# Nine weight conversions instead of twelve, the last six gate/up weight tiles cast by POOL during their load, and swapped keys made by the load instead of by the store

## The chip, the cores and the metric

The kernel runs on the 8 cores of one Trainium2 chip. Each core takes 2 of the 16 batches and runs the same program; there is no traffic between cores. The time of a run is that of its slowest core, in microseconds (us). A core has a matrix engine (TensorE, PE in the profile), a vector engine (DVE), a scalar engine (ACT), a general engine (POOL) and SyncE (SP); 16 DMA engines move data between HBM and the on-chip memory SBUF. SP and POOL each issue DMAs in the order of their own instruction streams: a DMA that waits for a semaphore holds up everything behind it on that engine.

## The reference, cut to what matters

```python
x   = x + layernorm(attention(layernorm(x), Mq, Mk, Mv))
# attention, 8 heads, keys of 64: scores = q @ k.T / 8, softmax over the QUERIES (axis=1),
#   out = att @ v, with v of 128 per head
wg, wu, wd = w_gate.astype(f32) / 127, w_up.astype(f32) / 127, w_down.astype(f32) / 127   # int32 inputs
x   = x + layernorm((silu(layernorm(x) @ wg.T) * (layernorm(x) @ wu.T)) @ wd.T)
# x: (16, 2048, 1024) float32; w_gate, w_up: (3072, 1024) int32; w_down: (1024, 3072) int32
```

The softmax runs over the queries of one position, so what this "attention" needs at a time is small: for each of the 16 groups G of 256 rows, tiles K of keys and values come by, 16 tiles per group, 256 in all.

## The kernel before, in words

The 4096 rows of a core are cut into 8 blocks of 512. The program has two parts.

**Projections, blocks 0 to 7.** Rows of x are loaded as tiles of 128 (T = 0 to 31), normalized (`ln1`, L264 on), transposed into `xnT` and multiplied with Wq, Wk, Wv. From T = 20 on the transpose is a DMA issued by SP (`P.flip`, L78); SP's order puts it among the loads and stores of the other work. A block has 16 units: 0 to 3 make queries, 4 to 7 keys, 8 to 15 values. Queries, keys and values are stored to HBM (`qk_d`, `v_d`), SP again. From block 4 on, score and value units of the attention (`s_unit`, `av_unit`) run between the halves of the projection units.

The keys are needed in two forms, since a score matmul uses 64 partitions at a time: as they are, and with the upper and lower 64 partitions swapped. `qk_unit` stores three pieces side by side in each 3072-wide row of `qk_d`: queries, keys, and, with two stores of 64 partitions, the swapped keys. `load_qk` (L384) loads the whole row with one DMA per group.

**FFN, blocks n = 0 to 7.** For each of 24 weight tiles ht, `gate_unit` and `up_unit` use the tile `wgu` (gate and up weights, 128 x 2048 bf16, four buffers), then 16 `down_unit` parts use all of `wd_sb`. Attention units run between the halves of these units as well. `load_wgu(i)` (L508) brings tile i, counted over all blocks; the first 24 are block 0's. It is called when up unit i - 4 is through. The first down unit waits for the last of the 12 loads of `wd_sb`.

**Weights.** The inputs are int32 and the matmuls want bf16. A DMA issued by POOL can change the type as it moves data. `convert(c)` (L647) turns two gate/up tiles, 2 MB of int32 in HBM, into 1 MB of bf16 in HBM (`gu_bf`), from where SP loads them in every block. There are 12 conversions: four in the first 64 units (after units 22, 30, 40, 50), six at (block, unit) = (4, 12), (5, 6), (6, 0), (6, 6), (6, 12), (7, 2), and the last two behind tiles 2 and 5 of the first FFN block. The down weights are converted on their way into SBUF by 12 DMAs behind tiles 7 to 21 of that block (`load_wd`), and stay there. Each of these is issued on POOL behind a wait for TensorE's count at that place.

The order on TensorE, DVE and ACT is written out by the program with a clock of its own, and no cost in it depends on DMAs.

Of the kernel before, what the change touches and what calls it, by code (L numbers as in the profile page):

```python
# [9 lines left out]
BF16 = mybir.dt.bfloat16  # L10
# [7 lines left out]
NHT = 24  # L18
# [9 lines left out]
QUIET = 5  # L28
MM = 0.216
SPACE = 1.6  # L30


class Program:
# [87 lines left out]
def build():  # L121
    nc = bass.Bass("TRN2", target_bir_lowering=False, dynamic_dma_scratch_size=16384)
# [4 lines left out]
    gu_hbm = nc.dram_tensor("gu", [NHT, 128, 2048], I32, kind="ExternalInput").ap()  # L127
    wd_hbm = nc.dram_tensor("wd", [NHT, 128, 1024], I32, kind="ExternalInput").ap()
    out_hbm = nc.dram_tensor("out", [NB, 2048, D], F32, kind="ExternalOutput").ap()
    gu_bf = nc.dram_tensor("gu_bf", [NHT, 128, 2048], BF16, kind="Internal").ap()  # L130
    qk_d = nc.dram_tensor("qk_d", [16, 128, 3072], BF16, kind="Internal").ap()
    v_d = nc.dram_tensor("v_d", [NB * 16, 128, 1024], BF16, kind="Internal").ap()

    es = ExitStack()
    P = Program(nc, es)
# [11 lines left out]
    q_qks = [P.sem(f"q_qks{i}") for i in range(NBLK)]  # L147
    q_vs = [P.sem(f"q_vs{i}") for i in range(4)]
    q_qk = [P.sem(f"q_qk{i}") for i in range(2)]
    q_v = [P.sem(f"q_v{i}") for i in range(6)]  # L150
    q_x1 = [P.sem(f"q_x1{i}") for i in range(8)]
    q_x2T = [P.sem(f"q_x2T{i}") for i in range(8)]
    q_conv = [P.sem(f"q_conv{i}") for i in range(12)]
    q_wgu = [P.sem(f"q_wgu{i}") for i in range(4)]
    q_wd = P.sem("q_wd")
    q_out = [P.sem(f"q_out{i}") for i in range(8)]

# [150 lines left out]
    qk_stored, v_stored = {}, {}  # L308

    def proj_units(blk, banks):  # L310

        par = blk % 2
        xT = xnT[par]
        qk_ev, v_ev = {}, {}
        turn = [0]

        def bank():
            turn[0] += 1
            return banks[turn[0] % len(banks)]

        def group(lhs, rhs, ready):
            name, ap = bank()
            done = None
            for dt in range(8):
                first = [bank_free.get(name), *ready] if dt == 0 else ()
                done = P.mm(ap, lhs(dt), rhs(dt), dt == 0, dt == 7, first, done=dt == 7)
                if dt == 3:
                    P.spent(4 * MM, 0.5)
            return name, ap, done

        def qk_unit(which, i):
            w, st = (wq, qst[par]) if which == 0 else (wk, kst[par])
            ready = [w_tok[which], *(xnT_tok[4 * blk + j] for j in range(4))]
            name, ap, done = group(lambda dt: w[:, 512 * dt + 128 * i:512 * dt + 128 * (i + 1)],
                                   lambda dt: xT[:, 512 * dt:512 * (dt + 1)], ready)
            dst = bass.AP(st, 256 * i, [[2048, 128], [1024, 2], [1, 256]])
            prev = [qk_stored[blk - 2]] if blk >= 2 else []
            qk_ev[i] = bank_free[name] = evac(dst, ap, done, *prev)
            if i == 3:
                ev = [qk_ev[n] for n in range(4)]  # L340
                row = 2 * blk * 128 * 3072
                if which == 0:
                    P.dma("sync", bass.AP(qk_d.tensor, row, [[3072, 128], [128 * 3072, 2], [1, 1024]]),
                          bass.AP(st, 0, [[2048, 128], [1024, 2], [1, 1024]]), q_qks[blk], *ev)
                    return
                P.dma("sync", bass.AP(qk_d.tensor, row + 1024,
                                      [[3072, 128], [128 * 3072, 2], [1, 1024]]),
                      bass.AP(st, 0, [[2048, 128], [1024, 2], [1, 1024]]), q_qks[blk], *ev)
                for half in range(2):
                    qk_stored[blk] = P.dma(  # L350
                        "sync", bass.AP(qk_d.tensor, row + 2048 + 64 * half * 3072,
                                        [[3072, 64], [128 * 3072, 2], [1, 1024]]),
                        bass.AP(st, 64 * (1 - half) * 2048, [[2048, 64], [1024, 2], [1, 1024]]),
                        q_qks[blk], *ev)

        def v_unit(j, c2):
            ready = [w_tok[2], xnT_tok[4 * blk + j]]
            name, ap, done = group(lambda dt: xT[:, 512 * dt + 128 * j:512 * dt + 128 * (j + 1)],
                                   lambda dt: wv[:, 1024 * dt + 512 * c2:1024 * dt + 512 * (c2 + 1)],
                                   ready)  # L360
            if j == 3 and c2 == 1:
                proj_done[blk] = done
            half, hh = j % 2, j // 2
            st = vst[2 * par + half]
            dst = bass.AP(st, 1024 * c2 + 128 * hh, [[2048, 128], [256, 4], [1, 128]])
            v_ev[j, c2] = bank_free[name] = evac(dst, ap, done, v_stored.get((blk - 2, half)))
            if hh == 1 and c2 == 1:
                b, k4 = blk // 4, blk % 4
                v_stored[blk, half] = P.dma(
                    "sync", bass.AP(v_d.tensor, (16 * b + half) * 131072 + 256 * k4,  # L370
                                    [[1024, 128], [2 * 131072, 8], [1, 256]]),
                    bass.AP(st, 0, [[2048, 128], [256, 8], [1, 256]]), q_vs[2 * par + half],
                    *(v_ev[half + 2 * a, c] for a in range(2) for c in range(2)))

        units = [lambda w=w, i=i: qk_unit(w, i) for w in range(2) for i in range(4)]
        units += [lambda j=j, c=c: v_unit(j, c) for j in range(4) for c in range(2)]
        return units
# [4 lines left out]
    x2T_tok, s_at = {}, [0.0]  # L382

    def load_qk(G):  # L384
        qk_tok[G] = P.dma("sync", qk[G % 2][:, :], qk_d[G, :, :], q_qk[G % 2],
                          qk_stored[G // 2], s_done.get(16 * (G - 2) + 15))

    def load_v(K):
        b, t = K // 128, K % 16
# [117 lines left out]

    def load_wgu(i):  # L508
        ht = i % NHT
        wgu_tok[i] = P.dma("sync", wgu[i % 4][:, :], gu_bf[ht, :, :], q_wgu[i % 4],  # L510
                           conv_tok[ht // 2], wgu_read.get(i - 4), *(xl_idle if i < 4 else ()))

    def gate_unit(n, ht):
        i = NHT * n + ht
        w, xT = wgu[i % 4], x2T[n % 2]
        for dt in range(8):
# [4 lines left out]
            if dt == 3:  # L521
                P.spent(4 * MM, 0.5)
        t_ = th[i % 2]
        tanh = P.act(lambda s: s.activation(t_[:, :], F[0][:, :], AF.Tanh, scale=1.0 / 254.0),  # L524
                     done, th_read.get(i - 2), *(th_idle if i < 2 else ()))

        def finish():
            bank_free["F0"] = gated[i] = P.dve(lambda v: v.scalar_tensor_tensor(  # L528
# [116 lines left out]
        turn(T)  # L645

    def convert(c, *waits):  # L647
        conv_tok[c] = P.dma("gpsimd", gu_bf[2 * c:2 * c + 2, :, :], gu_hbm[2 * c:2 * c + 2, :, :],
                            q_conv[c], *waits)

    wide = [(f"O{i}", Op[i // 2][:, 512 * (i % 2):512 * (i % 2 + 1)]) for i in range(4)]
    narrow = [(f"F{i}", F[i][:, :]) for i in range(2)]
# [6 lines left out]
    norm_at = {0: 4, 1: 5, 2: 6, 3: 7, 13: 8, 14: 9, 15: 10, 16: 11,  # L659
               25: 12, 26: 13, 27: 14, 28: 15, 34: 16, 36: 17, 38: 18, 40: 19}  # L660
    turn_at = {24: 8, 25: 9, 26: 10, 27: 11, 33: 12, 34: 13, 35: 14, 36: 15, 49: 16, 51: 17, 53: 18, 55: 19}
    early_conv = {22: 0, 30: 1, 40: 2, 50: 3}
    later_conv = {(4, 12): 4, (5, 6): 5, (6, 0): 6, (6, 6): 7, (6, 12): 8, (7, 2): 9}
    for u, unit in enumerate(first + rest):
        if u == 8:
            for T in range(4, 8):
# [44 lines left out]
        dst = bass.AP(wd, 2 * c * 1024, [[NHT * 1024, 128], [1024, 2], [1, 1024]])  # L711
        wd_tok[:] = [P.dma("gpsimd", dst, src, q_wd, *ramp_idle, *waits)]

    first_block = {2: lambda *w: convert(10, *w), 5: lambda *w: convert(11, *w)}
    for c in range(12):
        first_block[7 + 4 * c // 3] = lambda *w, c=c: load_wd(c, *w)

# [55 lines left out]
```

How the kernel before makes its waits and increments, by code:

```python
                def body(eng, ops=self.ops[name]):  # L105
                    seen = {}
                    for waits, fn, inc, amt in ops:
                        for s, v in waits:
                            if seen.get(s, 0) < v:
                                seen[s] = v
                                eng.wait_ge(self.h[s], v)
                        if fn is None:
                            continue
                        made = fn(eng)
                        if inc is not None:
                            made.then_inc(self.h[inc], amt)
```

## Time and profile before

| | us |
|---|---|
| median of 3 runs | 1765.6 |
| lowest, highest | 1762.24, 1766.82 |
| the profiled execution's own time | 1772.76 |
| its span, slowest core (4) | 1771.0 |
| fastest core of it (2) | 1747.3 |
| TensorE busy on core 4 | 1693.3 (96%) |

The span is the time from the first to the last instruction of a core; the run's time is a little longer. The profile page is that of core 4. The granted TensorE clock was 0.99 to 1.00 of full speed on every core. The DMA line of the page, which gives the mean busy share of the 16 DMA engines in 40 slices of 44 us, reads `9899999789934553465435543555255525441421`: the engines are near full in the first 11 slices, about 490 us, and half idle after that. DMA bytes are counted where they are written: a conversion or a load of down weights reads twice what the profile counts. Busy shares of different queues can overlap and add to more than one.

### The profile page before, as it was taken

The page shows a single profiled execution, that of the slowest core. Times are in us where ns is not written, and L with a number is a line of the kernel's source. Part 1 is how long each engine was busy: PE and PEld are TensorE (multiplying, and loading weights), DVE is VectorE, ACT ScalarE, POOL GpSimd, SP SyncE. Part 2 cuts the span into 40 slices and gives each one's busy share as a digit, 9 for nine tenths or more (in the row PEclk, how much of TensorE's full clock was granted, in tenths as well). Part 3 has the DMA queues.
Part 4 walks back from the last instruction along what each step waited for, and adds up shares of the span by engine and source line. Part 5 has one row for each costly group of instructions (what it writes and reads, how often), then busy time and mean ns, then how long its engine had stood idle before and what let it go on. Part 6 is the DMA issues. An engine that isn't in the chain of part 4 may idle for free.

```text
span 1771.0 us, 31869 instructions; the slowest of 8 cores (1747.3 to 1771.0 us)
## 1 busy us (share of the span) xinstructions
PE 1693.3 (96%) x10912; PEld 799.9 (45%) x10912; DVE 849.6 (48%) x1904; ACT 854.0 (48%) x1447; POOL 125.9 (7%) x245
## 2 busy tenths in 40 slices
PE   5999986998999999999999999999999999999997
PEld 2444442444444444444444444444444444444443
DVE  3434462535454545545454536463646354635433
ACT  3443553655545554555455545554555455552111
POOL 2110010001010001000010001000100010001000
PEclk9999998999999999999999999999999999999999
DMA  9899999789934553465435543555255525441421
GB/s 197 198 201 253 222 224 150 214 189 240 258 123 142 190 159 132 129 199 155 143 114 199 154 159 102 194 150 174 85 185 176 173 93 170 158 162 48 155 95 48
DMA packets 157518, 288.35 MB, mean 163 GB/s; under 512 B 56624, under 2 KB 75056, under 8 KB 156976
## 3 DMA queue, kind: packets, MB, share of 16 engines
q1 hardware_dynamic: 150400, 263.24, 48.5%
q0 software_dynamic: 6960, 23.07, 9.9%
q8 instruction: 91, 1.49, 0.3%
q14 instruction: 67, 0.55, 0.1%
HBM read 260.05 MB, written 50.33 MB: 175 GB/s over the span
## 4 chain that ended last, share of the span: by engine, by line
PE 83%; DVE 6%; DMA 5%; issue 2%; ACT 2%; SPq 1%; POOL 1%; DVEq 0%; POOLq 0%; ACTq 0%
PE F L71 58%; PE Op L71 17%; PE Sp L71 8%; DMA xnT<-xn 2%; DVE bnB L225 1%; DVE bnB L226 1%; DMA wgu<-gu_bf 1%; DMA wk<-mk 1%; ACT E L419 1%; ACT y L244 1%; SPq L78 1%; DMA wd_sb<-wd 1%; DVE th L528 1%; DMA xl<-x 0%; DVE mvB L227 0%
## 5 line engine op out<-in xcount | busy, mean ns | idle before, releaser
L419 ACT ACTIVATE E<-Sp 128x1024 bf16<-128x1024 f32 x512 | 523.8, 1023 | 625.9 <-PE Sp L71 625.7
L71 PE MATMUL F<-x2T,wgu 128*128 128x512 bf16 x3072 | 780.0, 380 | 20.3 <-DVE th L528 16.1
L71 PEld LDWEIGHTS F<-x2T,wgu 128*128 128x128 bf16 x3072 | 256.8, 98 | 307.6 <-issue 109.0
L71 PE MATMUL F<-wd_sb,hT 128*128 128x512 bf16 x1536 | 365.7, 380 | 0.7 <-DMA wd_sb<-wd 0.5
L71 PEld LDWEIGHTS Op<-vt,E 128*128 128x128 bf16 x4096 | 270.9, 98 | 122.5 <-issue 7.8
L71 PE MATMUL Op<-vt,E 128*128 128x128 bf16 x4096 | 313.7, 220 | 0.8 <-DVE vt L429 0.8
L528 DVE SCALAR_TENSOR_TENSOR th<-th,F 128x512 f32<-128x512 f32 x192 | 131.9, 687 | 259.8 <-ACT th L524 259.8
L551 DVE TENSOR_TENSOR hT<-th,F 128x512 bf16<-128x512 f32 x192 | 131.8, 686 | 180.1 <-PE F L71 176.2
L71 PEld LDWEIGHTS F<-wd_sb,hT 128*128 128x128 bf16 x1536 | 137.7, 98 | 157.3 <-issue 23.9
L71 PE MATMUL Sp<-qk 64*128 64x512 bf16 x1024 | 200.1, 387 | 2.4 <-ACT E L419 1.5
L429 DVE TENSOR_SCALAR vt<-vt,rsx 128x1024 bf16<-128x1024 bf16 x256 | 125.4, 490 | 53.9 <-DVE rsx L428 45.9
L524 ACT ACTIVATE th<-F 128x512 f32<-128x512 f32 x192 | 114.5, 596 | 73.3 <-PE F L71 73.0
L71 PEld LDWEIGHTS Sp<-qk 64*128 64x128 bf16 x1024 | 49.7, 92 | 216.0 <-issue 215.0
L419 ACT ACTIVATION_READ_ACCUMULATOR E<-Sp 128x1 f32 x512 | 99.6, 194 | 0.0
L248 DVE TENSOR_TENSOR x<-x,y 128x1024 f32<-128x1024 f32 x64 | 78.1, 1223 | 34.2 <-ACT y L244 33.7
L230 POOL TENSOR_TENSOR rsB<-vfB,mhalf 128x1 f32<-128x1 f32 x64 | 41.4, 647 | 572.4 <-DVE vfB L228 562.5
L584 DVE BATCH_NORM_STATS2 bnC<-y 128x6 f32<-128x512 f32 x64 | 44.3, 692 | 70.3 <-ACT y L577 67.7
L589 POOL TENSOR_TENSOR rsC<-vfC,mhalf 128x1 f32<-128x1 f32 x32 | 18.5, 578 | 702.4 <-DVE ssum L426 495.8
L244 ACT ACTIVATE y<-y,nbC,rsC 128x1024 f32<-128x1024 f32 x32 | 39.7, 1240 | 59.2 <-POOL nbC L240 57.6
L71 PE MATMUL F<-wv,xnT 128*128 128x512 bf16 x256 | 66.0, 380 | 0.4 <-DVE ssum L426 0.4
L579 DVE COPY y<-F 128x512 f32<-128x512 f32 x32 | 22.1, 690 | 81.0 <-PE F L71 80.9
L71 PE MATMUL Op<-wv,xnT 128*128 128x512 bf16 x256 | 56.7, 379 | 0.9 <-DVE kst L304 0.8
(65 smaller groups left out, 832.2 us busy)
## 6 DMA issues: line engine op xcount, KB each, us to landing
wgu<-gu_bf SPq DMA_DIRECT2D x192, 512.0 KB, 4.2
vt<-v_d SPq DMA_DIRECT2D x256, 256.0 KB, 4.6
xl<-x SPq DMA_DIRECT2D x32, 512.0 KB, 9.0
x<-x SPq DMA_DIRECT2D x32, 512.0 KB, 5.9
out<-x SPq DMA_DIRECT2D x32, 512.0 KB, 2.7
gu_bf<-gu POOLq DMA_DIRECT2D x12, 1024.0 KB, 14.4
qk<-qk_d SPq DMA_DIRECT2D x16, 768.0 KB, 6.1
v_d<-vst SPq DMA_DIRECT2D x16, 512.0 KB, 12.0
```

The lines of the kernel that those rows point to most:

```text
L71: "tensor", lambda t: t.matmul(out, lhsT, rhs, start=start, stop=stop),
L230: return P.pool(lambda g: g.tensor_tensor(rs[:, s:s + 1], vf[:, s:s + 1], mhalf[:, 0:1], AL.pow), t, const_done)
L244: return P.act(lambda a: a.activation(dst[:, :], y[:, :], AF.Identity, bias=nb[:, s:s + 1], scale=rs[:, s:s + 1]), *waits)
L248: return P.dve(lambda v: v.tensor_tensor(xt[:, :], xt[:, :], y[:, :], AL.add), *waits)
L419: lambda s: s.activation(e[:, 1024 * c:1024 * (c + 1)], Sp[:, :], AF.Exp, scale=0.125, accum_out=accx[:, a:a + 1]), done, av_tok.get(K - 4))
L429: vs_tok[K] = P.dve(lambda v: v.tensor_scalar(v_[:, :], v_[:, :], rsx[:, s:s + 1], None, AL.mult), t, v_tok[K])
L524: tanh = P.act(lambda s: s.activation(t_[:, :], F[0][:, :], AF.Tanh, scale=1.0 / 254.0), done, th_read.get(i - 2), *(th_idle if i < 2 else ...
L528: bank_free["F0"] = gated[i] = P.dve(lambda v: v.scalar_tensor_tensor(t_[:, :], t_[:, :], 1.0, F[0][:, :], AL.add, AL.mult), tanh)
L551: lambda v: v.tensor_tensor(dst, t_[:, :], F[1][:, :], AL.mult), done, gated[i],
L579: t = P.dve(lambda v: v.tensor_copy(y[:, 512:1024], F[1][:, :]), done, busy)
L584: b = P.dve(lambda v: v.bn_stats(bnC[:, o:o + 6], y[:, lo:lo + 512]), t)
L589: b = P.pool(lambda g: g.tensor_tensor(rsC[:, s:s + 1], vfC[:, s:s + 1], mhalf[:, 0:1], AL.pow), b, const_done)
```

## The change

It has three parts.

- Nine conversions instead of twelve: three in the first 64 units (after 22, 34, 46), six at (4, 14), (5, 8), (6, 2), (6, 11), (7, 2), (7, 9), none in the FFN. They cover tiles 0 to 17.
- Tiles 18 to 23 of the first FFN block are loaded by POOL straight from the int32 input into `wgu`, cast on the way. At gate unit i of these, SP stores the tile from SBUF to `gu_bf` (`keep_wgu`), for the seven later blocks. The next load into that buffer waits for the store.
- `qk_d` has rows of 2048: queries and keys. The two stores of swapped keys per block are gone; `load_qk` makes the swap with two loads of 64 partitions beside the load of 2048 columns.

```diff
+CONV = 18
...
+    def keep_wgu(i):
+
+        conv_tok[i] = P.dma("sync", gu_bf[i, :, :], wgu[i % 4][:, :], q_keep[i], wgu_tok[i])
...
     def load_wgu(i):
         ht = i % NHT
-        wgu_tok[i] = P.dma("sync", wgu[i % 4][:, :], gu_bf[ht, :, :], q_wgu[i % 4],
-                           conv_tok[ht // 2], wgu_read.get(i - 4), *(xl_idle if i < 4 else ()))
+        spill = [conv_tok[i - 4]] if CONV <= i - 4 < NHT else []
+        if CONV <= i < NHT:
+            wgu_tok[i] = P.dma("gpsimd", wgu[i % 4][:, :], gu_hbm[ht, :, :], q_wgc[i % 4],
+                               wgu_read[i - 4], *spill)
+        else:
+            wgu_tok[i] = P.dma("sync", wgu[i % 4][:, :], gu_bf[ht, :, :], q_wgu[i % 4],
+                               conv_tok[ht], wgu_read.get(i - 4), *spill, *(xl_idle if i < 4 else ()))
...
     def load_qk(G):
-        qk_tok[G] = P.dma("sync", qk[G % 2][:, :], qk_d[G, :, :], q_qk[G % 2],
-                          qk_stored[G // 2], s_done.get(16 * (G - 2) + 15))
+
+        buf, ready = qk[G % 2], [qk_stored[G // 2], s_done.get(16 * (G - 2) + 15)]
+        P.dma("sync", buf[:, 0:2048], qk_d[G, :, :], q_qk[G % 2], *ready)
+        for lo in (0, 64):
+            qk_tok[G] = P.dma("sync", buf[lo:lo + 64, 2048:3072], qk_d[G, 64 - lo:128 - lo, 1024:2048],
+                              q_qk[G % 2], *ready)
...
-                for half in range(2):
-                    qk_stored[blk] = P.dma(
-                        "sync", bass.AP(qk_d.tensor, row + 2048 + 64 * half * 3072,
-                                        [[3072, 64], [128 * 3072, 2], [1, 1024]]),
-                        bass.AP(st, 64 * (1 - half) * 2048, [[2048, 64], [1024, 2], [1, 1024]]),
-                        q_qks[blk], *ev)
...
-    early_conv = {22: 0, 30: 1, 40: 2, 50: 3}
-    later_conv = {(4, 12): 4, (5, 6): 5, (6, 0): 6, (6, 6): 7, (6, 12): 8, (7, 2): 9}
+    early_conv = {22: 0, 34: 1, 46: 2}
+    later_conv = {(4, 14): 3, (5, 8): 4, (6, 2): 5, (6, 11): 6, (7, 2): 7, (7, 9): 8}
...
-    first_block = {2: lambda *w: convert(10, *w), 5: lambda *w: convert(11, *w)}
+    first_block = {}
```

At gate unit i with 18 <= i < 24 the changed program calls `keep_wgu(i)`. The instructions of TensorE, DVE and ACT stand in the same order before and after. What moves stands on POOL and SP.

POOL in blocks 6 and 7 of the projections and the start of the FFN, before. `rsA` is the root for `ln1` (here T = 28 to 31), `rsB` and `nbB` belong to the attention's layernorms, `gu_bf<-gu` is a conversion:

```order
L75 DMA gu_bf<-gu 32x16384
L230 TENSOR_TENSOR rsB<-vfB,mhalf 128x1 x2
L230 TENSOR_TENSOR rsA<-vfA,mhalf 128x1 x2
L75 DMA gu_bf<-gu 32x16384
L230 TENSOR_TENSOR rsA<-vfA,mhalf 128x1
L75 DMA gu_bf<-gu 32x16384 x2
L230 TENSOR_TENSOR rsB<-vfB,mhalf 128x1
```

The same place now:

```order
L76 DMA gu_bf<-gu 32x16384
L233 TENSOR_TENSOR rsB<-vfB,mhalf 128x1 x2
L233 TENSOR_TENSOR rsA<-vfA,mhalf 128x1 x3
L76 DMA gu_bf<-gu 32x16384 x2
L233 TENSOR_TENSOR rsB<-vfB,mhalf 128x1
```

The conversion that stood between the last roots is gone, and all three come before the next one.

SP in block 6 of the projections, before. `kst` holds the keys, `xnT1<-xn2` and `xnT1<-xn3` are the last two transposes of the projections:

```order
L78 DMA_TRANSPOSE xnT1<-xn2 128x8x128
L75 DMA vt2<-v_d 128x1024
L75 DMA qk_d<-kst0 128x2x1024
L75 DMA qk_d<-kst0 64x2x1024 x2
L75 DMA vt3<-v_d 128x1024
L78 DMA_TRANSPOSE xnT1<-xn3 128x8x128
```

The same place now:

```order
L79 DMA_TRANSPOSE xnT1<-xn2 128x8x128
L76 DMA vt2<-v_d 128x1024
L76 DMA qk_d<-kst0 128x2x1024
L76 DMA vt3<-v_d 128x1024
L79 DMA_TRANSPOSE xnT1<-xn3 128x8x128
```

Two stores of swapped keys no longer stand ahead of the last transpose.

POOL in the second half of the first FFN block, before. `wd_sb<-wd` is a load of down weights with its cast, `rsC` belongs to the layernorm behind the FFN:

```order
L75 DMA wd_sb<-wd 128x2x1024
L230 TENSOR_TENSOR rsB<-vfB,mhalf 128x1 x2
L75 DMA wd_sb<-wd 128x2x1024 x8
L589 TENSOR_TENSOR rsC<-vfC,mhalf 128x1
L240 TENSOR_SCALAR nbC<-mvC,rsC 128x1
```

The same place now, with the weight tiles 18 to 23 in the buffers `wgu2`, `wgu3`, `wgu0`, `wgu1`, `wgu2`, `wgu3`:

```order
L233 TENSOR_TENSOR rsB<-vfB,mhalf 128x1 x2
L76 DMA wd_sb<-wd 128x2x1024 x2
L76 DMA wgu2<-gu 128x2048
L76 DMA wgu3<-gu 128x2048
L76 DMA wd_sb<-wd 128x2x1024
L76 DMA wgu0<-gu 128x2048
L76 DMA wd_sb<-wd 128x2x1024
L76 DMA wgu1<-gu 128x2048
L76 DMA wd_sb<-wd 128x2x1024
L76 DMA wgu2<-gu 128x2048
L76 DMA wgu3<-gu 128x2048
L76 DMA wd_sb<-wd 128x2x1024 x3
```

Six casts stand among the last loads of down weights; the last three loads come behind all of them. On SP the six loads of these tiles from `gu_bf` are gone and six stores `gu_bf<-wgu` stand at the gates of tiles 18 to 23.

## Rows read from the trace of the kernel before

**Rows 1.** The page's part 1, busy us by engine, core 4:

```profile
PE 1693.3 (96%) x10912; PEld 799.9 (45%) x10912; DVE 849.6 (48%) x1904; ACT 854.0 (48%) x1447; POOL 125.9 (7%) x245
```

**Rows 2.** The cores: span, mean granted clock of TensorE:

```profile
core 1: 1760.6 us, clock 0.993
...
core 4: 1771.0 us, clock 0.990
...
core 7: 1769.8 us, clock 0.991
```

**Rows 3.** Waits of TensorE, core 4: us in total, times, longest:

```profile
PE F L71 <- DMA xnT<-xn: 17.3, 2, 16.4
...
PE F L71 <- DMA wgu<-gu_bf: 3.7, 1, 3.7
```

**Rows 4.** The same of core 7 (two rows) and core 1:

```profile
PE F L71 <- DMA xnT<-xn: 14.5, 2, 11.9
...
PE F L71 <- DMA wgu<-gu_bf: 4.4, 1, 4.4
...
PE F L71 <- DMA wgu<-gu_bf: 5.7, 1, 5.7
```

**Rows 5.** Timeline of SP, core 4: start us, us on SP, what:

```profile
235.60 0.56 SPq L75 DMA_DIRECT2D qk<-qk_d  x1
...
267.27 10.97 SPq L78 DMA_TRANSPOSE xnT<-xn  x1
...
282.39 1.62 SPq L78 DMA_TRANSPOSE xnT<-xn  x1
```

**Rows 6.** Timeline of POOL, core 4; in brackets idle before, released by:

```profile
265.51 0.55 POOL L75 DMA_DIRECT2D gu_bf<-gu  x1 [1.22 <-PE Sp L71]
274.57 0.56 POOL L230 TENSOR_TENSOR rsA<-vfA,mhalf 128x1 f32<-128x1 f32 x1 [8.51 <-DVE vfA L228]
283.18 0.55 POOL L75 DMA_DIRECT2D gu_bf<-gu  x1 [8.04 <-PE Op L71]
...
389.95 0.49 POOL L75 DMA_DIRECT2D gu_bf<-gu  x1 [15.03 <-PE Op L71]
...
450.39 0.72 POOL L75 DMA_DIRECT2D wd_sb<-wd  x1 [11.35 <-PE Op L71]
455.60 0.71 POOL L75 DMA_DIRECT2D wd_sb<-wd  x1 [4.49 <-PE Op L71]
```

**Rows 7.** DMA issues, core 4, 283 to 284 us: count, median us to landing:

```profile
xnT<-xn SPq DMA_TRANSPOSE x1, 25.7
```

**Rows 8.** Timelines of SP and of POOL, core 0:

```profile
278.98 1.61 SPq L78 DMA_TRANSPOSE xnT<-xn  x1
...
280.45 0.55 POOL L75 DMA_DIRECT2D gu_bf<-gu  x1 [7.49 <-PE Op L71]
```

**Rows 9.** DMA issues, core 0, 276 to 286 us:

```profile
xnT<-xn SPq DMA_TRANSPOSE x1, 4.3
```

**Rows 10.** The chain that ended last, core 4: start us, us, what:

```profile
394.26 19.43 DMA wgu<-gu_bf
...
481.61 10.19 DMA wd_sb<-wd
```

**Rows 11.** DMA queues (packets, MB, share of engines) and issues, core 4, 440 to 490:

```profile
q1 hardware_dynamic: 4953, 8.54, 54.5%
q0 software_dynamic: 2126, 4.13, 50.3%
...
wd_sb<-wd POOLq DMA_DIRECT2D x6, 512.0 KB, 11.1
```

**Rows 12.** DMA queues, core 4, 480 to 490 us:

```profile
q1 hardware_dynamic: 694, 2.04, 53.8%
q0 software_dynamic: 512, 1.01, 53.4%
```

**Rows 13.** DMA issues of the whole page, core 4:

```profile
qk_d<-kst SPq DMA_DIRECT2D x8, 512.0 KB, 7.1
```

More of the change, by code:

```diff
@@ L130, in build @@
     gu_bf = nc.dram_tensor("gu_bf", [NHT, 128, 2048], BF16, kind="Internal").ap()
-    qk_d = nc.dram_tensor("qk_d", [16, 128, 3072], BF16, kind="Internal").ap()
+    qk_d = nc.dram_tensor("qk_d", [16, 128, 2048], BF16, kind="Internal").ap()
     v_d = nc.dram_tensor("v_d", [NB * 16, 128, 1024], BF16, kind="Internal").ap()
@@ L152, in build @@
     q_x2T = [P.sem(f"q_x2T{i}") for i in range(8)]
-    q_conv = [P.sem(f"q_conv{i}") for i in range(12)]
+    q_conv = [P.sem(f"q_conv{i}") for i in range(CONV // 2)]
+    q_keep = [P.sem(f"q_keep{i}") for i in range(NHT)]
     q_wgu = [P.sem(f"q_wgu{i}") for i in range(4)]
+    q_wgc = [P.sem(f"q_wgc{i}") for i in range(4)]
     q_wd = P.sem("q_wd")
@@ L340, in qk_unit @@
                 ev = [qk_ev[n] for n in range(4)]
[L341 to L348, printed above, removed]
-                for half in range(2):
-                    qk_stored[blk] = P.dma(
-                        "sync", bass.AP(qk_d.tensor, row + 2048 + 64 * half * 3072,
-                                        [[3072, 64], [128 * 3072, 2], [1, 1024]]),
-                        bass.AP(st, 64 * (1 - half) * 2048, [[2048, 64], [1024, 2], [1, 1024]]),
-                        q_qks[blk], *ev)
+                row = 2 * blk * 128 * 2048 + 1024 * which
+                qk_stored[blk] = P.dma(
+                    "sync", bass.AP(qk_d.tensor, row, [[2048, 128], [128 * 2048, 2], [1, 1024]]),
+                    bass.AP(st, 0, [[2048, 128], [1024, 2], [1, 1024]]), q_qks[blk], *ev)
         def v_unit(j, c2):
@@ L525, in gate_unit @@
                      done, th_read.get(i - 2), *(th_idle if i < 2 else ()))
+        if CONV <= i < NHT:
+            keep_wgu(i)
         def finish():
@@ L647, in convert @@
     def convert(c, *waits):
-        conv_tok[c] = P.dma("gpsimd", gu_bf[2 * c:2 * c + 2, :, :], gu_hbm[2 * c:2 * c + 2, :, :],
-                            q_conv[c], *waits)
+        conv_tok[2 * c] = conv_tok[2 * c + 1] = P.dma(
+            "gpsimd", gu_bf[2 * c:2 * c + 2, :, :], gu_hbm[2 * c:2 * c + 2, :, :], q_conv[c], *waits)
     wide = [(f"O{i}", Op[i // 2][:, 512 * (i % 2):512 * (i % 2 + 1)]) for i in range(4)]
```

## The prediction

> **What bounds the kernel now.** I read the page's busy shares first. TensorE is busy 1693.3 of 1771.0 us [rows 1], so only what makes it wait can move the time, and there are 78 us of that. The view of the cores came next: the slowest, core 4, needs 1771.0 us and core 1 needs 1760.6 [rows 2]. All run the same program on as much data, so this spread is waiting and not work. The waits of TensorE say which: on core 4 it waits 17.3 us for a transposed tile xnT and 3.7 us for a weight tile wgu [rows 3]; core 7 shows 14.5 and 4.4 us of the same two, core 1 only the weight tile, 5.7 us [rows 4]. Both are DMA waits of the first 420 us, the stretch in which the weights are converted.
>
> The timelines show how the xnT wait arises. On core 4 POOL issues a conversion at 265.51 us [rows 6]; SP then spends 10.97 us in the transpose it issues at 267.27, so the last transpose of the projections goes out only at 282.39 [rows 5]. The next conversion goes out at 283.18, 0.8 us behind it [rows 6], and the transpose lands after 25.7 us [rows 7]. On core 0 the same transpose goes out at 278.98 and the conversion at 280.45, 1.5 us behind [rows 8]; there it lands after 4.3 us [rows 9] and TensorE does not wait. The last two pieces of the chain: the weight tile asked for at 394.26 takes 19.43 us, beside a conversion issued at 389.95; the last down weights, asked for at 481.61, take 10.19 us and land at 491.80 [rows 6, 10]. The chain runs through that load, so the first down matmul started on its landing: the end of the first FFN block has no room left.
>
> **Part by part.**
>
> *Fewer conversions beside the transposes (gain).* TensorE's, DVE's and ACT's order is unchanged. Between (4, 12) and (6, 12) five conversions become four, in block 6 three become two, at units 2 and 11. The two swapped-key stores of 256 KB per block go: 8 x 0.5 = 4 MB. POOL's casts hold the 16 engines 6.1 us a MB (50.3% of 50 us for 4.13 MB [rows 11]), so a conversion of 1.05 MB holds them 6.4; with blocks 4 to 6 giving up 1.5 MB, that is 6.4 us and some 5 us (1.5 MB at 305 GB/s, the rate of 2.04 + 1.01 MB in 10 us [rows 12]), about 11 us of 150 us of saturated DMA. What matters more is the place: no conversion stands at unit 6 any more, so the transpose that blocked SP for 10.97 us is free. The last transpose's input is ready when POOL has its root at 274.57 [rows 6] and one DVE step more; SP can issue it near 277 us instead of 282.39. The conversion now behind unit 11 instead of 12 comes one unit earlier, about 2.9 us (17.67 us from 265.51 to 283.18 for six units, [rows 6]), near 280.2. The lead of 3 us is more than core 0's 1.5. I take the xnT wait as gone, bounds 0 and 17.3 us on core 4.
>
> *No conversion in the first FFN block (gain).* The two behind tiles 2 and 5, the second issued at 389.95, go, 12.8 us of DMA time by the same price, right where the late weight tile of 19.43 us stands. The wgu wait goes: 3.7 us on core 4, 4.4 on core 7, 5.7 on core 1; bounds 0 and these.
>
> *What the two are worth together* is set by the slowest core: core 4 1771.0 - 17.3 - 3.7 = 1750.0; core 7 1769.8 - 14.5 - 4.4 = 1750.9; core 1 1760.6 - 5.7 = 1754.9. The maximum falls from 1771.0 to 1754.9, by 16.1 us, not by core 4's 21.0.
>
> *Block 7 has two conversions, not one* (units 2 and 9). Nobody waits for the second until tile 16, whose gate stands beside POOL's issue at 450.39 [rows 6], over 100 us later; while it runs only tiles 0 to 3 and value tiles six steps ahead are loaded. I cost it at 0; if that cover fails it is one weight wait as on core 4, 3.7 us.
>
> *The last six weight tiles cast by POOL on their way in (loss).* Each is issued behind up unit i - 4, three tiles (15.6 us: POOL's issues behind successive tiles at 450.39 and 455.60 are 5.2 us apart, [rows 6]) before its gate. They need room on engines that have none. Between 440 and 490 us core 4 moves 8.54 MB on the hardware queue and 4.13 MB of down weights, which are read as int32, so 2 x 4.13: 16.8 MB in 50 us, 336 GB/s [rows 11]. The best 10 us of it, 480 to 490, carry 2.04 + 2 x 1.01 = 4.06 MB, 406 GB/s [rows 12]. The change adds six casts (6 x 1.05 MB read) and six keeping stores (3.1 MB), and takes out six plain loads (3.1 MB): 23.1 MB. At 336 GB/s that is 68.8 us, 18.8 over; at 406 it is 56.9, 6.9 over. The last down weights are behind all of it in POOL's queue and are waited for the moment they land, so the overrun comes out as TensorE idling. Lower end 0: the keeping stores and the tiles for block 1 (some 5 MB) are nobody's concern in this block, and if they were served last, 18 MB fit. A gain is excluded, since nothing gets less here. I take 9 us, near the end that the loaded engines showed. Two further waits are inside it. The cast of tile 22 waits for up unit 18, 5.2 us after gate 18 starts, and now also for the store of tile 18, issued as gate 18 starts; a 512 KB store lands in 7.1 us [rows 13], so the cast goes out 1.9 us later, and that of tile 23 the same; behind them in POOL's queue stand only casts and down weights. SP waits for each tile before it stores it, but gate i waits for the same; behind SP stand value tiles needed six steps later.
>
> Here a rule of the skill speaks against the change. The Trainium skill (HBM Reference, Specifications) gives a core about 358 GB/s when both of a pair stream. The same 23.1 MB would need 64.5 us by it, 14.5 over instead of 9, and the forecast would be some 5 us later. The trace's 406 GB/s over 10 us is above the rule, its 336 over 50 us below.
>
> *Three key loads instead of one:* 14 groups of steady state with two more issues of 0.56 us on SP [rows 5] are some 16 us of SP time, spread over a queue that waits for TensorE. Cost 0; without that cover a value tile is asked for 1 us late, six steps ahead of use. The same bytes are loaded.
>
> **Sum.** -16.1 + 0 + 9 = -7.1 us. Against the profiled execution (span 1771.0, its time 1772.8) that is 1765.7. It lies 7.2 us above the median of the runs, 1765.6, which are the measure: 1758.5, and I say 1758.
>
> **The rivals.**
>
> *The last transpose meets the conversion (slower).* Its place is block 6, unit 11. If SP issues the transpose less than about 1 us before the conversion or after it, it lands after some 25 us instead of 4. For: the conversion comes 2.9 us earlier on every core, and core 0 issued its transpose only 1.5 us ahead of the old one [rows 8]. Against: SP is not blocked at unit 6 any more. Then cores 4 and 7 gain nothing there, and all others lose 16 us: core 4 1771.0 - 3.7 + 9 = 1776.3, so +5.3 and 1771. It decides when the lead falls below 1 us.
>
> *The casts queue up (slower).* From 445 us (one tile before POOL's issue at 450.39 [rows 6]) to 482 us POOL issues twelve transfers, each as large as a down load. If one takes 5.7 us instead of the 3.2 us that 6.1 us a MB give [rows 11], the last lands at 445 + 12 x 5.7 = 513.4, 22 us after 491.8: -16 + 22 = +6, 1771.6. For: landings of 11.1 us already [rows 11]. Against: two issued at each other's heels still kept step. It decides above (491.8 - 445) / 12 = 3.9 us each.
>
> *The casts are hidden (faster).* The engines serve the urgent transfers within the 15.6 us of lead: -16.1, 1749.5. For: the lower bound above. Against: the chain ends in a down load that is only just in time [rows 10].
>
> *The relief is half, no change.* The profiled execution is 7.2 us above the median, so part of its xnT wait may be its own: -8 + 9 = +1, 1766.6.
>
> **How the numbers follow.** Forecast 35%, transpose meets conversion 15%, casts queue up 18%, casts hidden 17%, half relief 15%. About 0.3%, 5.3 us, is what a measurement can tell from no change: 1760.3 to 1770.9. The forecast's own spread, 1751 to 1766, gives 28 points to faster and 7 to the same; the hidden casts give 17 to faster; half relief 12 to the same and 3 to slower; the transpose rival 4 to the same and 11 to slower; the queue rival 18 to slower. Faster 0.45, same 0.23, slower 0.32. The range 1744 to 1778 leaves out the case of both losses at once (about 1784) and of more relief than the waits show.
>
> **What would show it.** Right: no xnT wait above 3 us on any core; SP's transposes in block 6 each under 4 us; no wgu wait near 400 us; instead waits for wgu and wd_sb between 470 and 505 us of 5 to 15 us on most cores, casts landing in 10 to 17 us; the spread of the cores under 15 us. Wrong: a 10 to 16 us xnT wait at the start of block 7 on most cores (first rival); wd_sb landing more than 20 us after its issue, or a wgu wait at every tile from 18 on (second); neither wait, with all cores near 1750 (third).

## The result and the profile after

The changed kernel takes 1784.1 us (median of 5 runs) against 1765.6 before: ratio 1.0095, 95% interval 1.0062 to 1.0127. A second comparison, in another session (e9), gave 1.0053 (1.0024 to 1.0082). It is slower, by 0.5 to 1%. Runs in which a lowered clock disturbed one die are left out of all ratios and of the medians below. The prediction said 1758, faster.

The page's part 1 of the changed kernel, core 5, the slowest, shows the same work in a longer span (first line), and the DMA queues moved 4 MB less (part 3: packets, MB, share of 16 engines):

```profile
span 1780.7 us, 31897 instructions; the slowest of 8 cores (1757.3 to 1780.7 us)
...
PE 1694.4 (95%) x10912; PEld 800.0 (45%) x10912; DVE 850.1 (48%) x1904; ACT 854.1 (48%) x1447; POOL 126.9 (7%) x248
...
q1 hardware_dynamic: 150656, 259.04, 48.1%
q0 software_dynamic: 7680, 23.07, 9.5%
```

The cores are spread as widely as before, but over other cores [rows 2]: the rows give span and mean granted clock.

```profile
core 1: 1771.8 us, clock 0.989
core 2: 1779.3 us, clock 0.987
...
core 4: 1757.3 us, clock 0.995
core 5: 1780.7 us, clock 0.987
...
core 7: 1760.5 us, clock 0.993
```

TensorE's waits on core 5, the counterpart of [rows 3] (us in total, times, longest): the xnT wait of 17.3 us is gone from the top, a wgu wait of 18.0 stands in its place, and two more have grown: before, no core waited more than 0.6 us for x2T or more than 3.1 for wd_sb.

```profile
PE F L72 <- DMA wgu<-gu_bf: 18.0, 1, 18.0
...
PE F L72 <- DMA x2T<-x: 5.3, 1, 5.3
PE F L72 <- DMA wd_sb<-wd: 5.0, 1, 5.0
```

The first matmuls on `wgu` and on `wd_sb` divide the span into three. On core 5 they start at 343.9 and 498.9 us (in the rows, behind the count, the ns of one, then first and last start):

```profile
L72 PE MATMUL F<-x2T,wgu x3072: 376/379/634, 343.9 to 1729.8; 128*128 128x512 bf16 x192
...
L72 PE MATMUL F<-wd_sb,hT x1536: 376/379/634, 498.9 to 1771.3; 128*128 128x512 bf16 x192
```

Before, on core 4, they started at 358.0 and 491.9. So the slowest core gained 14.1 us up to the first gate, lost 21.1 from there to the first down unit (155.0 us against 133.9) and 2.7 behind it: +9.7, the difference of the spans 1780.7 and 1771.0. These are two different cores. In the mean of all eight, the first gate starts at 343.4 us, where it started at 343.0, so nothing was gained ahead of it; the part between gate and down unit went from 136.6 to 143.7 us, and the part behind it from 1279.2 to 1281.1. Why that last part grew is open.

Where the 18 us arise is seen in the second half of the first FFN block. The chain of core 5 (start, us, what) has three long pieces there. The load issued at 428.46, right behind the transposes x2T, is that of tile 17, a plain load by SP. It takes 26.17 us. TensorE began to wait for it at 436.87 (454.87 - 18.00), 8.4 us behind its issue: the 15.6 us of lead had been cut to 8.4, since SP issues the load only behind the two transposes.

```profile
424.01 4.35 SPq L79
428.46 26.17 DMA wgu<-gu_bf
484.02 14.75 DMA wd_sb<-wd
```

And TensorE's wait for it (timeline):

```profile
454.87 1.87 PE L72 MATMUL F<-x2T,wgu 128*128 128x512 bf16 x4 [18.00 <-DMA wgu<-gu_bf]
```

What runs beside it, first on POOL, then on SP (timelines, start us, us on the engine, what; in brackets idle before, released by):

```profile
419.91 1.45 POOL L76 DMA_DIRECT2D wd_sb<-wd  x2 [0.25 <-PE Op L72]
426.58 0.57 POOL L76 DMA_DIRECT2D wgu<-gu  x1 [5.22 <-PE Op L72]
431.78 0.54 POOL L76 DMA_DIRECT2D wgu<-gu  x1 [4.63 <-PE Op L72]
432.30 0.71 POOL L76 DMA_DIRECT2D wd_sb<-wd  x1
```

```profile
421.95 6.41 SPq L79 DMA_TRANSPOSE x2T<-x  x2
428.46 3.70 SPq L76 DMA_DIRECT2D wgu<-gu_bf  x1
```

And the DMA of that stretch, core 5, 420 to 440 us: the mean rate, the queues, and the issues with count, size and median us to landing.

```profile
DMA packets 2253, 1.81 MB, mean 91 GB/s; under 512 B 1652, under 2 KB 1652, under 8 KB 2251
...
q0 software_dynamic: 630, 1.38, 62.9%
q1 hardware_dynamic: 1621, 0.42, 42.0%
...
wd_sb<-wd POOLq DMA_DIRECT2D x4, 512.0 KB, 18.5
wgu<-gu POOLq DMA_DIRECT2D x3, 512.0 KB, 21.3
...
wgu<-gu_bf SPq DMA_DIRECT2D x1, 512.0 KB, 26.2
x2T<-x SPq DMA_TRANSPOSE x2, 22.6
```

The engines are busy and move 91 GB/s, counted where it is written. POOL's casts hold them 12.6 us (62.9% of 20) for 1.38 MB, 9.1 us a MB, where the prediction reckoned 6.1 from [rows 11]: 4.8 us for a transfer of 0.52 MB instead of 3.2. The two transposes take 22.6 us; before, the two at this place took 8.7 on core 4, 7.3 to 13.7 on six others and 18.4 on core 6.

The schedule alone does not make this. POOL issues the same casts at the same distances from the transposes on all eight cores, and only cores 1, 2 and 5 are slow: there the transposes land in 18.0 to 22.6 us and the load of tile 17 in 18.3 to 26.2. On the five others they land in 8.2 to 11.2 and 8.5 to 11.9 us. Core 7, 417 to 437 us, the same stretch of its program:

```profile
DMA packets 3496, 3.92 MB, mean 196 GB/s; under 512 B 2225, under 2 KB 2225, under 8 KB 3495
...
q0 software_dynamic: 828, 2.10, 67.6%
q1 hardware_dynamic: 2667, 1.80, 34.2%
...
x2T<-x SPq DMA_TRANSPOSE x2, 8.4
```

The engines are as busy and move twice as much. But the run's time is that of its slowest core, so a delay that strikes some of the eight is paid in full.

### The profile page after: what moved, and what is told of

Same layout as the page of the kernel before. It is cut to its first block, busy times and chain, and to the rows that moved or that the text cites. A ratio compares the mean times of both kernels' runs of the same rounds, so it can differ in the third digit from the quotient of the medians.

```text
span 1780.7 us, 31897 instructions; the slowest of 8 cores (1757.3 to 1780.7 us)
## 1 busy us (share of the span) xinstructions
PE 1694.4 (95%) x10912; PEld 800.0 (45%) x10912; DVE 850.1 (48%) x1904; ACT 854.1 (48%) x1447; POOL 126.9 (7%) x248
## 4 chain that ended last, share of the span: by engine, by line
PE 82%; DVE 6%; DMA 5%; issue 3%; ACT 2%; SPq 1%; POOL 1%; DVEq 0%; POOLq 0%; ACTq 0%
PE F L72 57%; PE Op L72 17%; PE Sp L72 8%; DMA wgu<-gu_bf 1%; DVE bnB L228 1%; DVE bnB L229 1%; DMA vt<-v_d 1%; DMA wk<-mk 1%; ACT E L416 1%; DMA wd_sb<-wd 1%; ACT y L247 1%; SPq L79 1%; DMA xl<-x 1%; DVE th L536 1%; DVE mvB L230 0%
## 5 line engine op out<-in xcount | busy, mean ns | idle before, releaser
L536 DVE SCALAR_TENSOR_TENSOR th<-th,F 128x512 f32<-128x512 f32 x192 | 132.0, 688 | 280.2 <-ACT th L530 280.0
L597 POOL TENSOR_TENSOR rsC<-vfC,mhalf 128x1 f32<-128x1 f32 x32 | 18.4, 576 | 709.7 <-DVE ssum L423 503.1
```

The lines of the kernel that those rows point to most:

```text
L597: b = P.pool(lambda g: g.tensor_tensor(rsC[:, s:s + 1], vfC[:, s:s + 1], mhalf[:, 0:1], AL.pow), b, const_done)
```

## The experiments

Ratios are to the kernel before on the same chip and in the same session, with 95% intervals. Kernels e1 to e4, e5 to e8 and e9 to e12 each ran together.

**e1: the key part alone.** The changed kernel with before's twelve conversions, no casts of tiles:

```diff
-CONV = 18
+CONV = 24
-    early_conv = {22: 0, 34: 1, 46: 2}
-    later_conv = {(4, 14): 3, (5, 8): 4, (6, 2): 5, (6, 11): 6, (7, 2): 7, (7, 9): 8}
+    early_conv = {22: 0, 30: 1, 40: 2, 50: 3}
+    later_conv = {(4, 12): 4, (5, 6): 5, (6, 0): 6, (6, 6): 7, (6, 12): 8, (7, 2): 9}
-    first_block = {}
+    first_block = {2: lambda *w: convert(10, *w), 5: lambda *w: convert(11, *w)}
```

> The key part alone: rows of 2048 in qk_d, swapped keys made by two more loads, with the twelve conversions at their places in the kernel before and no cast in the FFN. My theory after the result (the loss is in the first FFN block, from the six casts) expects this part harmless: 1758 to 1767 us against 1765.6 before, no wait at the first FFN tile. The rival that the two extra loads per group or the smaller store have a price of their own expects 1772 or more.

Measured: 1765.1 us, ratio 0.998 (0.9951 to 1.001). No wait for keys of more than 0.4 us on any core. The key part is harmless, and its 4 MB less buy nothing that can be told from zero.

**e2: no casts, the new places.** `CONV = 24`, and the last three conversions in the FFN:

```diff
-    first_block = {}
+    first_block = {1: lambda *w: convert(9, *w), 3: lambda *w: convert(10, *w), 5: lambda *w: convert(11, *w)}
```

> The changed kernel without its casts: nine conversions in the projections at their new places, the last three as conversions behind tiles 1, 3 and 5 of the first FFN block, new keys. If the six casts cause the loss, this is 1755 to 1768 us, with the x2T wait of 4 to 6 us at the first gate still there (it would belong to the conversion at block 7, unit 9) and a wgu wait of up to 10 us near tile 10. If the new places of the conversions cause it, this stays at 1775 or above.

Measured: 1777.3 us, ratio 1.0055 (1.0034 to 1.0076). Without any cast of a tile, 0.55% of loss is there, as much as the changed kernel showed in its second comparison. The x2T wait is 3.4 to 6.2 us on all eight cores, the wgu wait 6.5 to 12.8 (near tile 9; for loads of 24 to 27 us on cores 0, 1 and 6). So my theory of the moment, that the casts are all of it, fell: the places of the conversions cost as well. This run could not say which place, since it has a ninth conversion in block 7 and a third in the FFN.

**e3: no keeping stores.** The casts stay; `keep_wgu` and the waits on it go, and tiles 18 to 23 reach `gu_bf` by three conversions during the down units of the first block.

```diff
-        if CONV <= i < NHT:
-            keep_wgu(i)
...
+                if n == 0 and j < 3 and part == 0:
+                    convert(9 + j, ("c_tensor", P.count["c_tensor"]))
```

> The changed kernel with the six casts but without the six keeping stores and the waits on them; tiles 18 to 23 reach gu_bf by three conversions in the down phase of the first block instead. If the volume of stores and the waits of the casts on them are the loss, the time falls to 1768 or less and the wait for wd_sb goes. If the casts themselves are what blocks the engines beside SP's transposes (tile 17's load landing in 18 to 26 us, issued before any store), the waits for wgu at tile 17 stay and the time stays at 1776 to 1784.

Measured: 1779.6 us, ratio 1.0068 (1.004 to 1.0096). The wgu wait for tile 17 was still 20.7 us on core 7 and 12.8 on core 5. Stores and waits on them are not the loss; the late load is issued before any of them. The wd_sb wait did not go either, it grew to 9 to 11 us on five cores.

```profile
PE F L72 <- DMA wgu<-gu_bf: 20.7, 1, 20.7
...
PE F L72 <- DMA x2T<-x: 7.1, 1, 7.1
```

The rows are TensorE's waits on core 7 of this run.

**e4: down weights earlier,** behind tiles 2 to 13:

```diff
-        first_block[7 + 4 * c // 3] = lambda *w, c=c: load_wd(c, *w)
+        first_block[2 + c] = lambda *w, c=c: load_wd(c, *w)
```

> The changed kernel with the twelve down-weight loads behind tiles 2 to 13 instead of 7 to 21. The DMA engines show shares of 0.65 to 0.72 between 360 and 400 us in the changed kernel, so the loads fit there, and the casts then have POOL's queue for themselves. If the casts lose by meeting the down loads, the wait for wd_sb (4 to 6 us on every core) goes and the wgu waits fall: 1762 to 1772 us. If the casts lose against the transposes alone, only the wd_sb wait goes: 1774 to 1780.

Measured: 1780.3 us, ratio 1.0069 (1.0041 to 1.0097). The wd_sb wait is gone on all cores of the profiled execution, but that one was the fastest of eleven (1765.8), so its trace does not stand for the median; it shows wgu waits of 5.8 to 8.9 us on all eight cores instead, nearly all of it near tile 13 and at most 3.0 us for tile 17. Taking the down loads off the casts repaired nothing. Inconclusive as to where the time of the slower executions went.

**e5: the ninth conversion out of block 7.** The changed kernel with one conversion moved:

```diff
-    later_conv = {(4, 14): 3, (5, 8): 4, (6, 2): 5, (6, 11): 6, (7, 2): 7, (7, 9): 8}
+    later_conv = {(4, 14): 3, (5, 8): 4, (6, 2): 5, (6, 11): 6, (7, 2): 7}
-    first_block = {}
+    first_block = {0: lambda *w: convert(8, *w)}
```

> The changed kernel with its ninth conversion behind the first FFN tile instead of at block 7, unit 9. If that conversion is what holds up the transposes x2T ahead of the first gate (a wait of 1.5 to 5.6 us in the changed kernel, 0.6 at most before), the wait falls under 1 us on all cores, and the time by some 3 to 4 us, to about 1.0075 of before, unless the conversion costs as much in the FFN (a wgu wait near tile 4 to 6). A rival that the x2T wait comes from the three key loads in its place keeps the wait.

Measured: 1767.0 us, ratio 0.999 (0.9967 to 1.0014), so 0.6 to 1% less than the changed kernel, more than I expected. No x2T wait shows on any core. The first gate starts at 337.2 us in the mean of the cores, 343.4 in the changed kernel. The casts of tiles 18 and 19 are still there, and so is the wait for tile 17, on two cores (5.3 and 7.0 us).

**e6: four casts, the old places.** e1 with `CONV = 20` and nothing in the FFN but the casts of tiles 20 to 23:

```diff
-CONV = 24
+CONV = 20
-    first_block = {2: lambda *w: convert(10, *w), 5: lambda *w: convert(11, *w)}
+    first_block = {}
```

> Keys as in the change; ten conversions at the ten places of the kernel before, none in the FFN; only tiles 20 to 23 cast by POOL. The two casts issued beside the x2T transposes of the first FFN block (tiles 18 and 19) are plain loads again. If these two make the load of tile 17 late, its wgu wait (up to 18 us in the changed kernel) goes and the first FFN block takes about 137 us instead of 144: 1760 to 1768 us, ratio 0.996 to 1.002. If any cast costs its share of traffic at the end of the block, wd_sb waits of 4 us stay and the ratio is 1.004.

Measured: 1761.8 us, ratio 0.9947 (0.9928 to 0.9967): faster than before. No wait for a plain wgu load on any core, a wd_sb wait of 3.4 to 6.7 us on all.

**e7: six tiles not converted.** Tiles 18 to 23 are left out of the computation; tiles 12 to 17 are loaded in their place. The rest is the changed kernel.

```diff
         ht = i % NHT
+        ht = ht - 6 if ht >= 18 else ht
```

> The changed kernel with the conversion of tiles 18 to 23 left out altogether (tiles 12 to 17 are loaded in their place, by SP): no casts, no keeping stores. It prices the two halves of the change apart. By my theory that the casts cost 7 to 15 us and the new places of the conversions about nothing, it is 1755 to 1765 us, ratio 0.995. If the new places cost 9 us as the run without casts suggests, it stays at ratio 1.003 or above in spite of the work left out. First FFN block about 130 to 133 us.

Measured: 1757.9 us, ratio 0.9929 (0.9903 to 0.9955). From the first gate to the first down unit it takes 130.4 to 133.2 us. Against the changed kernel (1.0053, 1.0095 in its two comparisons) the casts, stores and their waits cost 1.2 to 1.7%, 22 to 29 us of the slowest core, though by the prediction's count they add only 6.3 MB of traffic. The two sides come from different sessions, each measured against the kernel before beside it.

**e8: short rows.** e1 with each conversion addressed as 128 x 2 x 2048 instead of 32 x 16384:

```diff
-            "gpsimd", gu_bf[2 * c:2 * c + 2, :, :], gu_hbm[2 * c:2 * c + 2, :, :], q_conv[c], *waits)
+            "gpsimd", bass.AP(gu_bf.tensor, 2 * c * 262144, [[2048, 128], [262144, 2], [1, 2048]]),
+            bass.AP(gu_hbm.tensor, 2 * c * 262144, [[2048, 128], [262144, 2], [1, 2048]]), q_conv[c], *waits)
```

> Keys as in the change, all twelve conversions at the places of the kernel before, each read in rows of 8 KB (128 x 2 x 2048) instead of 32 rows of 64 KB. If the long rows are what keeps SP's transposes and loads waiting beside a conversion, xnT lands sooner, the wgu waits of 5 to 7 us near tile 10 shrink, and the time falls to 1755 to 1762. If it is the volume that counts, nothing changes: 1762 to 1768 (ratio 0.998 as with the key part alone).

Measured: 1766.6 us, ratio 0.997 (0.994 to 0.9999), not to be told from e1's 0.998. So the length of the rows has no price of its own in this kernel's time. It does show on SP. Of the 16 transposes that SP issues next behind the conversions of (6, 0) and (6, 6), two on each core, ten held SP for 5.3 to 11.9 us in e1; in e8 none held it for more than 2.9. They landed about as late in both, after 8.3 to 15.3 us in e1 and 9.7 to 13.4 in e8. First e1, then e8, core 0:

```profile
242.86 11.91 SPq L79 DMA_TRANSPOSE xnT<-xn  x1
```

```profile
245.90 1.89 SPq L79 DMA_TRANSPOSE xnT<-xn  x1
```

Neither kernel has a conversion at (7, 9), so whether short rows would help there was not measured.

**e9: the changed kernel again,** without an edit.

> The changed kernel once more, unchanged, beside the kernel before and the three kernels of this group, since its ratio of 1.0095 came from another session. Expected 1.007 to 1.012. Were it below 1.003, the comparison with the run that moves one conversion out of block 7 (0.999) would be void.

Measured: 1779.3 us, ratio 1.0053 (1.0024 to 1.0082). Lower than the first 1.0095, with intervals that overlap. The wgu wait for tile 17 is there on five cores, 6.5 to 10.2 us.

**e10: e6 with the down weights two tiles sooner.**

```diff
-        first_block[7 + 4 * c // 3] = lambda *w, c=c: load_wd(c, *w)
+        first_block[5 + 4 * c // 3] = lambda *w, c=c: load_wd(c, *w)
```

> The kernel with four cast tiles and the old places (ratio 0.9947), its down-weight loads two tiles sooner, behind tiles 5 to 19, where no conversion stands any more. Its only large wait left is that for wd_sb, 3.4 to 6.7 us on every core. If the loads find room, the wait falls to 0 to 2 us and the ratio to about 0.992. If the engines are full from tile 5 on too, the wait turns into waits for wgu and the ratio stays at 0.995.

Measured: 1754.9 us, ratio 0.9927 (0.9895 to 0.9959), the fastest kernel of the study, 12.4 us below the kernel before. The cores' spans (1744.4 to 1750.3 us) lie within 6 us of each other, and the first FFN block takes 128.1 to 131.4 us to its down units:

```profile
core 0: 1750.3 us, clock 0.996
...
core 6: 1744.4 us, clock 0.995
```

**e11: a conversion at (7, 9) alone.** e1 with conversion 10 moved there from behind FFN tile 2:

```diff
-                  (7, 2): 9}
+                  (7, 2): 9, (7, 9): 10}
-    first_block = {2: lambda *w: convert(10, *w), 5: lambda *w: convert(11, *w)}
+    first_block = {5: lambda *w: convert(11, *w)}
```

> The kernel with the new keys and the old twelve conversions (ratio 0.998), one of them moved from behind FFN tile 2 to block 7, unit 9, no casts of tiles. If a conversion at (7, 9) by itself holds up the x2T transposes, the x2T wait at the first gate is 3 to 6 us on all cores, where it was 0.7 at most. The wgu wait of 5 to 7 us near tile 10 should shrink with one conversion less in the FFN, so the ratio is 0.997 to 1.003. If x2T does not wait, the wait of the changed kernel came from (7, 2) and (7, 9) together or from elsewhere.

Measured: 1772.2 us, ratio 1.0028 (1.0004 to 1.0053), 0.5% above e1. The x2T wait is 1.6 to 6.1 us on seven of the eight cores. The two timelines of SP and POOL show how, in this run's core 5; the second fence is the same place of e1, core 5, which has no conversion there.

```profile
321.36 0.58 POOL L76 DMA_DIRECT2D gu_bf<-gu  x1
...
331.11 10.59 SPq L79 DMA_TRANSPOSE x2T<-x  x2
```

```profile
334.31 2.57 SPq L79 DMA_TRANSPOSE x2T<-x  x2
```

With a conversion issued ten us earlier SP needs 10.59 us to issue the two transposes, without it 2.57, and everything behind them in SP's queue moves with them. On core 3 of this run, which shows no x2T wait and starts its first gate at 353.4 us all the same, what comes late is a value tile: the chain (start, us, what) has a load of 22.70 us issued at 316.94, and TensorE waits for the DVE step on that tile (timeline, in brackets the wait and its releaser).

```profile
316.94 22.70 DMA vt<-v_d
```

```profile
340.36 1.01 PE L72 MATMUL Op<-vt,E 128*128 128x128 bf16 x8 [5.95 <-DVE vt L426]
```

**e12: the casts beside the transposes alone.** The changed kernel, (7, 9) kept, with tiles 18 and 19 converted behind the first FFN tile and only 20 to 23 cast:

```diff
-CONV = 18
+CONV = 20
-    first_block = {}
+    first_block = {0: lambda *w: convert(9, *w)}
```

> The changed kernel, with the conversion at (7, 9) still there, but tiles 18 and 19 converted behind the first FFN tile instead of cast: only 20 to 23 are cast. If the two casts issued beside the x2T transposes are what makes the load of tile 17 land in 18 to 26 us, that wgu wait goes while the x2T wait at the first gate stays: ratio 1.001 to 1.004. If the conversion at (7, 9) alone explains the loss, the ratio stays at 1.007 or above.

Measured: 1767.5 us, ratio 1.0002 (0.9974 to 1.003), against 1.0053 of the changed kernel beside it. Plain wgu loads are waited for on no core; the x2T wait stays at 1.3 to 5.9 us on all. The transposes of group 3 landed in at most 9.6 us on all 24 cores of the profiles of e6, e7 and e12, which do not cast tiles 18 and 19; with these casts (the changed kernel, e9, e3, e5) 12 of 32 cores took more than 12 us. It takes no tile cast to slow them, though: two cores of the kernel before (13.7 and 18.4) and four of e11 (12.8 to 16.3) are above 12 us too, and on each of these six POOL issued a down load, also a cast, between 0.3 us ahead of the transposes and 1.2 us behind them. On core 2, whose transposes go out at 424.68, POOL's queue has down loads beside them and the first cast only at 439.72; the transposes land in 9.2 us and the weight loads behind them in 8.0 (both for 420 to 440 us):

```profile
wgu<-gu_bf SPq DMA_DIRECT2D x3, 512.0 KB, 8.0
...
x2T<-x SPq DMA_TRANSPOSE x2, 9.2
```

## Why the prediction was wrong

**TensorE's DMA waits of the first 500 us decide, and the slowest core is the one that collects them.** Right as far as the stretch goes. The page shows the same busy time, and the waits that differ lie there. But the forecast took the cores' gain from three of them: "The maximum falls from 1771.0 to 1754.9". Core 6 needs 1762.1 us, and its wait of 9.4 us is for tile 17, behind transposes that landed in 18.4 us. No term of the forecast removes that, so by its own terms the maximum falls to 1762.1, by 8.9 us and not 16.1, and with the 9 us of the casts the sum is about 0. The row also showed, before the change, the very wait that later decided:

```profile
440.99 1.44 PE L71 MATMUL F<-x2T,wgu 128*128 128x512 bf16 x3 [9.41 <-DMA wgu<-gu_bf]
```

**The xnT wait goes, because the last transpose leaves SP sooner.** Right that it goes, and that the transpose leaves SP sooner; the new places of the conversions were not what it took. In the changed kernel no core waits for xnT more than 3.2 us. On core 5, SP issues the last transpose at 276.18, forecast near 277, and POOL the conversion at 280.03, forecast 280.2; SP's transpose at unit 6 takes 1.22 us instead of 10.97 [rows 5]. First the two rows of SP, then POOL's:

```profile
267.06 1.22 SPq L79 DMA_TRANSPOSE xnT<-xn  x1
...
276.18 1.22 SPq L79 DMA_TRANSPOSE xnT<-xn  x1
```

```profile
280.03 0.55 POOL L76 DMA_DIRECT2D gu_bf<-gu  x1 [4.91 <-PE Op L72]
```

So the first rival, the transpose meeting the conversion, did not come about. (Its price had a slip: if all cores but 4 and 7 lose 16 us, core 1 comes to 1760.6 - 5.7 + 16 + 9 = 1779.9, above core 4's 1776.3.) But "What matters more is the place" is not borne out by e1, which has all conversions of block 6 at the old places. SP is held there just as long on some cores, 11.51 us on core 4:

```profile
265.13 11.51 SPq L79 DMA_TRANSPOSE xnT<-xn  x1
...
278.40 1.90 SPq L79 DMA_TRANSPOSE xnT<-xn  x1
```

Still the last transpose goes out 2.3 to 5.6 us ahead of the conversion on every core and lands in 4.7 to 6.8, and no core waits more than 0.3 us for xnT. What e1 shares with the change is that the two stores of swapped keys are gone; before, the three key stores together kept SP for 2.03 us on core 4 (next row), and one takes 0.37 in e1.

```profile
279.02 2.03 SPq L75 DMA_DIRECT2D qk_d<-kst  x3
```

The size is not shown either. e1 lacks the wait and is at 0.998, which cannot be told from no gain; the profiled execution of the kernel before was slower than the median by 7.2 us, as the rival of half relief had said. e7, which has all of the change but the casts, is at 0.9929, 12.7 us below the kernel before beside it, where the prediction without its 9 us would say 16.1. That the two are close does not divide the gain among its terms.

**The wgu wait near tile 10 goes with the two FFN conversions.** Right: it is gone from all cores of the changed kernel.

**"Block 7 has two conversions, not one. I cost it at 0."** Wrong, the smaller of the two failed steps that cost time. I asked who waits for the conversion, and who is loaded beside it, and did not list the two x2T transposes that SP issues some ten us behind it and that the first gate waits for. The value tiles, six steps ahead, were no cover either: one took 22.70 us in e11. A conversion there costs 0.5% in e11 against e1, some 8 us, where the two intervals together leave 2 to 15 (e11 also takes a conversion out from behind FFN tile 2, a relief); e5 without it is 0.6 to 1% below the changed kernel. My bound was 3.7 us. The collision I had described for xnT in block 6 simply moved to x2T in block 7.

**"I take 9 us" for the casts (0 to 18.8).** Wrong, the larger failed step, a mis-sized term: 22 to 29 us by e7. I priced it by volume at the rate of a loaded stretch, 336 to 406 GB/s. Two of the six casts, those of tiles 18 and 19, are issued beside the x2T transposes of group 3, and there the engines fell to 91 GB/s on core 5. e12 takes these two away and gets 0.5% back, some 9 us, and the plain-load wait for tile 17 is gone on all cores. That wait is what the slowest cores have: 18.0, 14.0 and 9.9 us on cores 5, 2 and 1.

The wd_sb wait that I had foreseen is there on every core, 4.2 to 5.7 us, at or under the low end of the 5 to 15 forecast. The casts of tiles 20 to 23, clear of the transposes, are not free: e12 still lies 0.7%, some 13 us, above e7, and from first gate to first down unit its cores take 136.5 us in the mean against 132.0. In e6 they stand beside a gain, because two conversions left the FFN for them.

The second rival, the casts queuing up, forecast a loss too (1771.6), but not for its reason. In the stretch that it spoke of, 445 to 485 us, the casts held the engines of core 5 for 6.1 us a MB (65.2% of 40 us for 4.26 MB), 3.2 us a transfer, under its threshold of 3.9; only in 420 to 440 us was it 4.8. Neither of its signs came (wd_sb landing more than 20 us after its issue, a wgu wait at every tile from 18 on), and with the stores (e3) or the down loads (e4) moved away the kernel stays at 1.007.

The rule I had weighed against the change agrees in direction only. The Trainium skill (HBM Reference, Specifications) gives about 358 GB/s per core, which made 14.5 us of the term. The trace shows 91 GB/s written where the time was lost on core 5; by the prediction's count, with casts taken twice, that is 3.2 MB in 20 us, 159 GB/s, less than half of that figure, so this core's share was not used up there.

The two failed steps add up. From the changed kernel's 1.0053 in the last group, 0.5% for (7, 9) and 0.5% for the two casts lead to 0.995, where e6, which has neither, was measured (0.9947).

**Three key loads instead of one at no cost.** Right (e1).

What stays open: why a cast issued by POOL slows SP's transposes, and loads behind them, so far beyond its bytes, and why it did so on three cores and not on the five others with the same schedule. Traffic of the other cores at that moment is a rival that no run separates. The keeping stores are ruled out by e3, since the late load is issued before any of them. e8 rules out row length as a cause of the late landings, not of SP being held. A kernel with the transposes taken away was not run. The gap between 1.0053 and 1.0095 for the same kernel is open too, as is e4's median.

## What to carry to other kernels

When a DMA is moved, list every DMA issued close behind it at its new place (here the transposes came 8 to 11 us behind the conversion), with who waits for each, and not only who waits for the one moved; the price here was set by two transposes, not by the bytes. Find the transposes in the SP stream first and keep casting DMAs away from them. Read the waits of all cores, and not only of the slowest: the one that is left sets the time. A load that is waited for on every core is worth asking for sooner: e10, with the same traffic as e6 but the down loads two tiles sooner, brought the wd_sb wait from 3.4 to 6.7 us down to 1.9 at most and is faster than the kernel before and the changed one. Against e6 (0.9927 and 0.9947) its ratio cannot be told apart.

## What the runs showed of the hardware

A transposing DMA took 3.0 us to land clear of a cast (core 5 of the changed kernel, issued at 276.18), and the two issued from 421.95 on beside casts on the same core took 22.6; with the same casts beside them, the two of core 7 took 8.4. Before the change the last transpose of the projections took from 4.3 to 25.7 us [rows 7, 9]. SP itself was held, 10.59 us in e11 against 2.57 in e1 for issuing two. Changing a conversion from 32 rows of 64 KB to 256 rows of 8 KB made no difference that could be measured in the kernel's time, but SP's transposes behind it held SP for at most 2.9 us, where up to 11.9 had been seen. Casts held the 16 engines 6.1 us a MB in one stretch [rows 11] and 9.1 in another.
